# Another order of work in an attention block between two mixtures of experts: layer normalisations one pair later, reordered end of attention, a third batch gathered on TensorE

## The reference

```python
x = x + 0.5 * ffn(layernorm(x))     # "first experts"
x = x + attn(layernorm(x))          # "attention"
x = x + 0.5 * ffn(layernorm(x))     # "last experts"

def ffn(inputs):                    # 2048 tokens, 8 experts, 128 -> 512 -> 128
    probs = softmax(tokens @ gate_w.T); expert = argmax(probs)        # one expert for a token
    ranks = cumsum(one_hot(expert)) - 1                               # its place in the expert
    kept if rank < 320                                                # capacity
    h = relu(dispatched @ w1 + b1); out = h @ w2 + b2
    ans = probs * out, put back to the tokens' rows
def attn(states):                   # 16 heads of 64, causal
    q, k, v = (tanh(states @ W + bias) for each of Wq, Wk, Wv)
    return tanh(softmax(q @ k.T / 8, causal) @ v @ Wo + bo)
```

## Time and profile before

| | us |
|---|---|
| median of three runs | 459.39 |
| lowest and highest run | 458.07, 459.64 |
| the profiled execution | 458.94 |
| its span | 457.2 |
| TensorE busy in the span | 401.2 (88%) |
| VectorE busy | 322.0 (70%) |
| ScalarE busy | 247.8 (54%) |
| GpSimd busy | 207.7 (45%) |

### The profile page before, as it was taken

The page is one execution under the profiler, slowest core; times in us unless marked ns, Lnnn a source line. Parts: engine busy times, 40 slices in busy tenths (PEclk is TensorE's granted clock), DMA queues, the critical chain, the costliest instruction groups (busy, mean ns, idle before and its releaser), DMA issues.

```text
span 457.2 us, 11460 instructions
## 1 busy us (share of the span) xinstructions
PE 401.2 (88%) x4654; PEld 302.2 (66%) x4654; DVE 322.0 (70%) x852; ACT 247.8 (54%) x369; POOL 207.7 (45%) x176
## 2 busy tenths in 40 slices
PE   1689889758799999999999999999999989789992
PEld 0556556526677888587877687887678875346771
DVE  6789677836999786389799478889558886554321
ACT  2111444228476878387768377777468661224641
POOL 6665064254544444154443357453346544130546
PEclk9999999989899999999999999999999999979997
DMA  7912643208000000000000010000000000217531
GB/s 213 373 49 75 177 124 94 62 24 279 2 1 1 3 2 4 1 24 1 3 2 3 8 30 7 10 1 3 7 8 30 10 1 19 58 31 204 146 96 36
DMA packets 25372, 25.46 MB, mean 56 GB/s; under 512 B 2664, under 2 KB 21551, under 8 KB 25048
## 3 DMA queue, kind: packets, MB, share of 16 engines
q1 hardware_dynamic: 21424, 18.33, 13.7%
q0 software_dynamic: 2304, 4.25, 2.8%
q10 hardware_dynamic: 1592, 2.14, 1.3%
HBM read 16.72 MB, written 9.58 MB: 58 GB/s over the span
## 4 chain that ended last, share of the span: by engine, by line
PE 60%; DVE 26%; issue 9%; POOL 2%; ACTq 1%; DMA 1%; ACT 1%; POOLq 0%; DVEq 0%
PE sc L820 8%; PE sc L680 7%; DVE Pl L1317 7%; PE pj L689 7%; DVE Ph L1312 6%; PE pj L789 5%; PE tT L869 5%; PE cx L852 4%; PE cx L854 3%; PE cx L853 3%; PE pj L799 3%; PE tT L623 3%; PE pj L820 2%; PE pj L869 2%; DVE XN L994 1%
## 5 line engine op out<-in xcount | busy, mean ns | idle before, releaser
L820 PE MATMUL sc<-Tq,Tk 64*128 64x128 f32 (+2 forms) x640 | 78.6, 345 | 0.0
L852 PE MATMUL cx<-Vh,Ph 128*128 128x65 f16 x640 | 65.8, 196 | 10.5 <-DVE Pl L1317 5.0
L820 PEld LDWEIGHTS sc<-Tq,Tk 64*128 64x128 f32 x640 | 62.3, 187 | 11.6
L1312 DVE CAST Ph<-Pf 128x1024 f16<-128x1024 f32 (+1 forms) x48 | 49.3, 1028 | 29.2 <-ACT Pf L568 29.2
L852 PEld LDWEIGHTS cx<-Vh,Ph 128*128 128x128 f16 x640 | 58.6, 98 | 16.5 <-DVE cn L1326 5.2
L853 PE MATMUL cx<-Vl,Ph 128*128 128x64 f16 x640 | 65.6, 194 | 0.0
L854 PE MATMUL cx<-Vh,Pl 128*128 128x65 f16 x640 | 65.3, 194 | 0.0
L853 PEld LDWEIGHTS cx<-Vl,Ph 128*128 128x128 f16 x640 | 59.0, 99 | 0.3
L854 PEld LDWEIGHTS cx<-Vh,Pl 128*128 128x128 f16 x640 | 59.2, 98 | 0.0
L479 ACT ACTIVATE hT<-sc,RT 128x320 f32<-128x320 f32 x64 | 33.7, 527 | 35.4 <-PE sc L680 34.9
L1312 DVE CAST Ph<-Wf 128x1024 f16<-128x1024 f32 (+1 forms) x48 | 42.8, 892 | 4.8 <-ACT Wf L568 4.7
(11 more groups left out here) (237 smaller groups left out, 1050.5 us busy)
## 6 DMA issues: line engine op xcount, KB each, us to landing
W<-in_L_ffn_w SPq DMA_DIRECT2D x32, 256.0 KB, 2.9
disp<-empty SPq DMA_DIRECT2D x2, 1320.0 KB, 7.9
XE<-disp SPq DMA_DIRECT2D x18, 132.0 KB, 2.6
X<-xmid SPq DMA_DIRECT2D x4, 256.0 KB, 3.2
out<-X SPq DMA_DIRECT2D x4, 256.0 KB, 2.3
XR<-disp SPq DMA_DIRECT2D x18, 33.0 KB, 2.3
X<-in_L_attn_states SPq DMA_DIRECT2D x2, 256.0 KB, 3.3
X<-in_L_attn_states SPq DMA_DIRECT2D x1, 512.0 KB, 5.4
```

Source lines behind the costliest of these rows:

```text
L820: m = mm(score_bank(h, c)[:, o + x:o + y], Tk[u][half(h), q:q + P], Tq[u][half(h), q + x:q + y], start=False, stop=last and (c, h) != (2, 0))
L852: mm(cx[:, o:o + HD + 1], Ph[u][:, h, a:a + P], Vh[u][:, kt, h, :], start=kt == 0, stop=False)
L1312: dve.tensor_copy(Ph[u][:, :, at], Pf[u][:, :, at]).then_inc(S["p_hi"], 1)
```

## The change

It has four parts.

1. `experts` on VectorE: weight split and bias step stand ahead of `outputs(e)`, `normalise_rows(e + 4)` behind it; the split has 6 pieces of 512 columns instead of 8 of 384. In the first experts TensorE's `gather(1)` is done for batch 0 ahead of hidden(0), the rest behind it.
2. X_STATS, X_APPLY and X_TURN are one pair later, and batch 0's scaling of batch 1's rows too: the scaling stands behind the casts of a pair. The transposes of xa wait for their tile alone; the first two terms of kq wait for the high half XH alone.
3. The tail: the scores of the last pair ahead of the ranks; the projection in groups of inputs 0 to 3, 4 to 6 and 7 instead of 0 to 5, 6 and 7; the last context in PSUM bank sc; on VectorE the work on batch 2 (ranks, part, weights, places, low half, one-hot matrices) behind `normalise`; on GpSimd the dispatch of batch 2 behind the power of batch 3.
4. Last experts: batch 2 of experts 0 and 1 is gathered on TensorE too (`gather_group`), the part is of batches 0 and 1 alone (loads wait for 24 scatters) and is added in PSUM by matmuls with the identity, so that `keep_part` and the addition are gone. 6 filling matmuls remain of 20. TensorE starts with gather(0), gather(1), hidden(0), hidden(1), outputs(0), outputs(1).

```diff
-X_STATS, X_APPLY, X_TURN = {0: 1, 2: 2, 4: 3}, {1: 1, 3: 2, 5: 3}, {2: 1, 4: 2, 6: 3}
-LATE, SPLIT = 5, 384
+X_STATS, X_APPLY, X_TURN = {1: 1, 3: 2, 5: 3}, {2: 1, 4: 2, 6: 3}, {3: 1, 5: 2, 7: 3}
+LATE, SPLITS = 5, 6
...
-        NH = flat(CT[:, 0:2, :]).rearrange("p (t d) -> p t d", d=P)
-        NL = Pl[0][:].rearrange("p a n -> p (a n)")[:, 0:NT * P].rearrange("p (t d) -> p t d", d=P)
-        HOT = [flat(Pf0[:]).rearrange("p (t n) -> p t n", n=CAP), flat(CT[:, 2:7, :]).rearrange("p (t n) -> p t n", n=CAP)]
-        part = [Tq[e][:, 0:CAP] for e in range(2)]
...
+        PART = (NG - 2) * GT
+        NH, NL = [tile[:].rearrange("p (t d) -> p t d", d=P) for tile in (XH, XL)]
+        hot_first = [flat(tile).rearrange("p (t n) -> p t n", n=CAP) for tile in (Pf[0][:], CT[:, 0:5, :])]
+        hot_last = [flat(tile).rearrange("p (t n) -> p t n", n=CAP) for tile in (Pf[0][:], Pf[1])]
+        HOT = (hot_first, hot_last)
+        gbank = (pj1, cx)
...
-                            sp.wait_ge(S["scattered"], 16 * (2 * NT - GT))
+                            sp.wait_ge(S["scattered"], 16 * (NT + PART))
...
-            batch_dispatch(NG - 2)
             batch_inv_std(NG - 1)
             for e in range(2):
                 pool.wait_ge(xe_in[e], 32)
             pool.wait_ge(xr_in[0], 64)
+            batch_dispatch(NG - 2)
             batch_dispatch(NG - 1)
...
-            def keep_part():
-
-                act.wait_ge(S["part_ps"], 1)
-                act.activation(part[0], pj1[:, 0:CAP], ACT.Copy)
-                act.activation(part[1][:, MAIN:CAP], pj1[:, CAP:CAP + REST], ACT.Copy)
-                act.activation(part[1][:, 0:MAIN], sc[0][:, 0:MAIN], ACT.Copy).then_inc(S["part_ready"], 1)
...
+            split_n(2 * NG - 2, NG - 2)
...
-            def transpose_group(src, ps, done):
+            def transpose_group(src, ps, done, ready=None):
                 for t in range(GT):
+                    if ready:
+                        pe.wait_ge(ready[0], ready[1] + t)
                     last = nc.tensor.transpose(ps[:, P * t:P * t + P], src[:, t, 0:P], identf[:])
                 last.then_inc(done, 1)
...
+            def gather_group(phase, e, g):
+
+                since = g - NG + 2
+                done = NG + since + 1 if phase else g + 1
+                pe.wait_ge(S["n_hi"], done)
+                pe.wait_ge(S["n_lo"], done)
+                pe.wait_ge(S["hot_ready"], 2 * NG + 2 * since + e + 1 if phase else NG * e + g + 1)
+                for t in range(GT * g, GT * g + GT):
+                    begin, final = t == (PART if phase else 0), t == NT - 1
+                    mm(gbank[e][:, 0:CAP], NH[:, t, :], HOT[phase][e][:, t, :], start=begin, stop=False)
+                    last = mm(gbank[e][:, 0:CAP], NL[:, t, :], HOT[phase][e][:, t, :], start=False, stop=final)
+                if final:
+                    last.then_inc(S["xe_ps"], 1)
...
-                gather(0)
-                hidden(0)
-                gather(1)
-                outputs(0)
-                hidden(1)
+                if phase:
+                    gather(0, (NG - 1,))
+                    gather(1, (NG - 1,))
+                    hidden(0)
+                    hidden(1)
+                    outputs(0)
+                    outputs(1)
+                else:
+                    gather(0, range(NG))
+                    gather(1, (0,))
+                    hidden(0)
+                    gather(1, range(1, NG))
+                    outputs(0)
+                    hidden(1)
                 tokens(2)
                 for e in range(1, E - 2):
                     hidden(e + 1)
                     turn_back(e - 1)
                     tokens(e + 2)
-                    outputs(e)
+                    if e > 1 or not phase:
...
-                pe.wait_ge(S["xa_ready"], g + 1)
                 if g:
                     pe.wait_ge(S["x_lo"], g)
-                transpose_group(xa, tT, S["xa_ps"])
+                transpose_group(xa, tT, S["xa_ps"], (S["xa_ready"], GT * g + 1))
...
-                    pe.wait_ge(S["x_lo"], b + 1)
+                    pe.wait_ge(S["x_hi"], b + 1)
...
+                        if r == 0 and w and xl:
+                            pe.wait_ge(S["x_lo"], b + 1)
...
-                if c or h:
+                if bank is cx and (c or h):
...
-            step(NG, 0, project=False, route=lambda: rank_batch(NG - 2, cx), cx_read=(S["rank_read"], NS + NG - 1))
             pairs = NPAIR * NG
+            scores(pairs - 1, 1, False)
+            pe.wait_ge(S["ctxn"], 2 * (pairs - 3) + 2)
+            rank_batch(NG - 2, cx)
+            pe.wait_ge(S["rank_read"], NS + NG - 1)
+            context(pairs - 2, 0, 0)
+            context_t(pairs - 3, 1)
+            context(pairs - 2, 0, 1)
             pe.wait_ge(S["tv"], pairs)
-            project_out(NG - 1, pj0, 0, 6)
+            project_out(NG - 1, pj0, 0, 4)
+            context(pairs - 1, 1, 0)
             context_t(pairs - 2, 0)
-            context(pairs - 1, 1, 0)
-            context(pairs - 1, 1, 1)
-            project_out(NG - 1, pj0, 6, 7)
+            context(pairs - 1, 1, 1, sc[0])
+            project_out(NG - 1, pj0, 4, 7)
             context_t(pairs - 1, 1)
             project_out(NG - 1, pj0, 7, 8)
             turn_out(NG - 1)
-            keep_busy(20)
+            for e in range(2):
+                gather_group(1, e, NG - 2)
+            pe.wait_ge(S["part_in"], 1)
+            for e in range(2):
+                rest = slice(REST * e, REST * e + REST)
+                for j in range(2):
+                    mm(gbank[e][:, P * j:P * j + P], XM[e][:, j, :], identf[:], start=False, stop=False)
+                last = mm(gbank[e][:, MAIN:CAP], XMR[rest, :], identf[rest, rest], start=False, stop=False)
+            last.then_inc(S["part_ps"], 1)
+            keep_busy(6, sc[0])
             pe.wait_ge(S["x_added"], NG)
             turn_batch(NG - 1)
             route_logits(NG - 1, sc[1])
-            pe.wait_ge(S["part_in"], 1)
-            for j in range(2):
-                nc.tensor.transpose(pj1[:, P * j:P * j + P], XM[0][:, j, :], identf[:])
-                nc.tensor.transpose(sc[0][:, P * j:P * j + P], XM[1][:, j, :], identf[:])
-            nc.tensor.transpose(pj1[:, MAIN:MAIN + P], XMR[:], identf[:]).then_inc(S["part_ps"], 1)
             rank_batch(NG - 1, sc[3])
...
+                    for dst, at, n in ((0, 0, CAP),) if e == 0 else ((REST, 0, MAIN), (0, MAIN, REST)):
+                        last = dve.tensor_copy(xeT[e][:, dst:dst + n], gbank[e][:, at:at + n])
...
-                    part = slice(SPLIT * e, SPLIT * e + SPLIT)
+                    part = slice(512 * e, 512 * e + 512)
...
-                if between:
-                    between()
                 for e in range(E):
                     if e + 2 < E:
                         tokens(e + 2)
-                    if e + 4 < E:
-                        normalise_rows(e + 4)
+                    if e == 0 and between:
+                        between()
                     if phase == 0:
-                        split_weights(e)
-                    outputs(e)
-                    if not phase:
+                        if e < SPLITS:
+                            split_weights(e)
                         if e == 1:
                             bias_high()
                         if e == 2:
...
                             where()
                         if e == 5:
                             bias_rows()
+                    outputs(e)
+                    if e + 4 < E:
+                        normalise_rows(e + 4)
...
-            step(NG, 0, between=lambda: take_ranks(s, NS + NG - 2, GT * (NG - 2), 0, GT, cx))
-            place(s, GT * (NG - 2), 0, GT)
+            step(NG, 0, between=lambda: read_ranks(s, NS + NG - 2, 0, GT, cx))
+            normalise_part()
             normalise(NPAIR * NG - 1, 1, 0)
-            normalise(NPAIR * NG - 1, 1, 1)
+            normalise(NPAIR * NG - 1, 1, 1, sc[0])
+            weigh(s, NS + NG - 2, GT * (NG - 2), 0, GT)
+            place(s, GT * (NG - 2), 0, GT, near=True)
+            low_n(NG, NG - 2)
+            dve.wait_ge(S["spot_ready"], NS + 1)
+            for e in range(2):
+                hot(1, e, NG - 2)
             add_out(NG - 1)
             batch_stats(NG - 1)
             norm_batch(NG, NG - 1)
-            normalise_part()
-            low_n(NG, NG - 1)
+            low_n(NG + 1, NG - 1)
             s = Steps(dve, S["route_step"], ROUTE_STEPS * (NS + NG - 1), ROUTE_STEPS)
             choose(s, NS + NG - 1, 0, GT, sc[1])
             take_ranks(s, NS + NG - 1, GT * (NG - 1), 0, GT, sc[3])
             place(s, GT * (NG - 1), 0, GT, near=True)
-            dve.wait_ge(S["spot_ready"], NS + 1)
+            dve.wait_ge(S["spot_ready"], NS + 2)
```

90 lines of the change are left out of this document (40 added, 50 removed).

## The result

The changed kernel takes 451.32 us (median of four runs, 450.07 to 452.66), the kernel before on the same chip 458.81: a ratio of 0.984 (95% interval 0.980 to 0.987), or 7.5 us less. The profiled execution took 452.66, with a span of 450.6; it was the longest of the four. So the table has both.

A forecast was written before the change was run, and what follows sets the result against it. No single engine was taken to bound the kernel, so each stage was read by itself: 458.94 - 4.0 - 3.1 - 1.3 + 0.7 = 451.2 us. The range of 8 in 10 was 447.8 to 455.2.

The forecast's parts named there:

- First experts: VectorE's new order closes TensorE's holes before the hidden layers, and the earlier gather helps: 4.0 us less, bounds 0.9 and 4.4.
- The 0.3 for a full VectorE: First experts: 0.3 us taken off the gain because VectorE's own load is full at expert 2.
- First batch: Attention's first batch: normalisations one pair later remove VectorE's wait for GpSimd's power: 3.1 us less, between 2.1 and 3.7.
- one pair later the power runs beside the first pair's casts: First batch: GpSimd's power runs during VectorE's casts, saving 1.17 + 0.9 = 2.1 us, the lower end.
- Rival A: One large term missing (22%): first experts keep 0.9 of 4.0, 454.3, or first batch 1.0 to 2.1 of 3.1, 452.2 to 453.3.
- The port: First batch: by the skill's shared-port rule the power would block a cast about 1 us, making 3.1 2.1; forecast kept 3.1.
- Tail: Attention's tail: earlier last contexts, fewer small steps and a bank of its own, less projection matmuls moved behind: 1.3 us less.
- the 1 to spare: Tail: VectorE gets some 6 us of work ahead of the last addition, leaving about 1 us of its idle time.
- Last experts: Both gathers first close one hole, but the copy of expert 3 is uncovered: 0.7 us more, between 0 and 1.4.
- the charge of 1.5 for the copy that outputs(1) no longer covers: Last experts: before hidden(3), outputs(0), scaling, copy and hand-overs take 1.7 us against 0.22, so 1.5 more.
- Rival D: Batches 1 to 3: pairs fall into another rhythm where VectorE's subtraction meets GpSimd's each time: 467 us (4%).

The follow-up runs named there:

- e1_vector_order: Changed kernel with VectorE's order in the first experts alone put back (scaling, split, outputs, bias step): 455.99 us, 0.9925; 455.79 without one execution of 690.21.
- second profile: Profiled execution of a later run of the changed kernel, same code, another granted clock: 449.0 us, span 446.9; that run's median 452.53 us, 0.9859.
- b1_tables_alone: Kernel before with only the changed X_STATS, X_APPLY and X_TURN tables, third chip: 461.45 us, 0.9954.
- e7_before_fill: Kernel before with the same 13 filler matmuls ahead of its attention and nothing else, second chip: 463.81 us, 1.0009.
- g1_fill_again: Changed kernel with the 13 fillers, a second time, on the third chip: 452.28 us, 0.9741.
- e8_more_fill: Kernel of e4 with 9 more fillers, 5 while VectorE chooses batch 3's experts, 4 while it makes the last one-hot matrices: 450.74 us, 0.9725.
- e3: Changed kernel with 13 more matmuls nobody reads, 10 behind the first experts' last product, 3 behind the transposes of batch 0's rows: 449.76 us, 0.9795.
- e4: Changed kernel with the 13 fillers and, in the last experts, TensorE's outputs(1) back behind tokens(3): 450.33 us, 0.972.
- e5: Changed kernel with the 13 fillers and the three old X_STATS, X_APPLY and X_TURN tables put back: 455.49 us, 0.9814.
- e6_fill_tail: Changed kernel with the 13 fillers, old projection groups in the tail and the last context's second half in the first's bank: 452.2 us, 0.9746.

## Why the prediction was right, and where it was not

**First experts: right.** 4.0 was forecast, 3.93 came. The four periods took 19.49 by the starts in the timeline (50.20 to 69.69), 19.66 by those in the chain, where 19.42 was forecast. Hidden(1) came 0.4 sooner instead of 0.9 (47.23 to 46.79). The earlier gather gave its 1.1 (from hidden(0) to hidden(1) it is 7.56 us, 8.72 before), but hidden(0) came 0.7 later and not 0.2; how much of that is the gather is open, since hidden(0) starts anywhere from 38.72 to 41.37 in the profiles with this order. The 0.3 for a full VectorE wasn't needed, so two small misses cancel. e1_vector_order confirms the mechanism.

**First batch: right mechanism, missed condition.** The step that failed is "one pair later the power runs beside the first pair's casts", with the casts taken as ready at once. At the full clock the term is 3.5 (3.1 forecast, 3.7 the upper bound). In the first profile it is 0.93, under the lower bound of 2.1: the first scores ran at 1.2 GHz, and VectorE waited 2.86 us for them where it had waited for GpSimd. Rival A had this ("a pair that is served sooner only waits later"), and priced what it takes away at 1.0 to 2.1; in the first profile 2.17 went. Before, VectorE's scaling stood ahead of the casts and covered that delay; when it goes, the cover goes. The low clock of 93.2 to 96.6 in the kernel before was a cost that only waited for its cover to be taken away.

**The port.** The forecast set a rule of the Trainium skill ("SBUF — State Buffer", Who interferes with whom) against the row of a cast beside GpSimd's power. In the second profile the power ran from 102.61 to 104.03, and VectorE's two casts beside it took 1.29 together:

```profile
102.61 1.42 POOL L358 TENSOR_TENSOR r<-ve,mhalf 128x4 f32<-128x4 f32 x1 [1.32 <-DVE ve L999]
104.02 2.96 POOL L403 TENSOR_TENSOR Pl<-Pf,Ph 128x1024 f16<-128x1024 f32 x1
```

That is 0.65 for each, as 0.68 in the row of before. They weren't blocked, and the rows decided rightly. The third cast, from 104.90, took 2.36 beside GpSimd's large subtraction where it takes 0.42 alone; that one agrees with the rule.

**Tail: right on the first chip.** 1.3 forecast, 1.56 came in the first profile: 0.60 ahead of the first projection and 0.96 behind it. VectorE still idled 1.45 us ahead of the last addition, near the 1 to spare that was forecast, and GpSimd 3.47 ahead of its last dispatches, against 3.

On the other two chips it is worth more, which nobody forecast. From the keys of pair 31 to the last addition the changed tail takes 27.90 to 27.95 us on all three chips, where the clock isn't low in it; the old one takes 29.51 in before, 31.98 in b1_tables_alone on the third chip and 33.17 in e7_before_fill on the second. Of that, 2.0 us stand at one place, VectorE's `normalise` of the first half of the last context. Its first instruction in before, and below it the same one in b1_tables_alone:

```profile
385.54 0.18 DVE L1322 RECIPROCAL rden<-cx 128x4 f32<-128x4 f32 x1 [2.25 <-PE cx L854]
```

```profile
388.10 0.18 DVE L1322 RECIPROCAL rden<-cx 128x4 f32<-128x4 f32 x1 [4.27 <-remote]
```

TensorE's part was done at 386.04 in the second case, and e7_before_fill has the same 4.27. "remote" is a release for which the trace has no instruction, so what VectorE waited for stays open.

**Last experts: wrong by 0.9.** The hole of "near 2 us" before hidden(3) came as forecast (2.07). What failed is first the clock of the gathers. The forecast let the second gather run in part at the lower level, 1.1 to 2.2 us, as the first did in before; but in the first profile both ran at the upper level, 2.33 us for the two where one alone had taken 2.30. With the clock low over the gathers as in before, the changed order takes 41.05 from the indices to the last hidden layer (g1_fill_again), 0.6 more than the 40.49 before, near the 0.7 that was forecast; at the full clock 40.29 and 39.96, which is less. And second, the charge of 1.5 for the copy that outputs(1) no longer covers is right only at the low clock, where outputs(1) in its old place is worth 1.4. At the full clock TensorE is sooner done and would wait for the loads of experts 2 and 3: hidden(2) starts at 12.42 in e8_more_fill with outputs(1) not yet done, and at 13.42 in the first profile with its 2.15 us done, so more than half of it fills that wait.

**The sum.** The first profile lost 2.2 in the first batch and gained 0.9 in the last experts, which leaves it 1.3 above the forecast; and it was the longest of the four executions, 1.34 above their median. That the median meets the forecast to 0.1 us is luck, though three of the four terms are right in mechanism and near in size in one profile or the other. Rival D did not come: from pair 8 to pair 31 it is 200.70 to 200.76 us in all traces of the first chip and 201.03 to 201.18 on the others, with the old tables and the new.

## What to carry to other kernels

Where a wait is removed, ask what else it covered: here a slow stretch of the clock ahead of it cost nothing while another engine was later, and 2.6 us once that engine was early. So read the granted clock of every stretch that feeds the place, not only of the stretch itself, and price a term at both levels. And an uncovered hole is only a cost if the engine could have been there sooner: look for the transfer that sets the next start. Compare two traces of a stage only where the clock takes the same course in both.

## What was not expected of the hardware

The granted clock takes different courses in the same kernel: low from 89.6 to 103.2 us in one execution and from 89.1 to 92.5 in another, with the same code. The span differs by 3.7 us (450.6 and 446.9). The 13 fillers went with the upper level ahead of the first scores in five profiles (e3, e4, e5, g1, e8), but not in e6_fill_tail (low from 94.8 to 98.2) nor in e7_before_fill; and e1_vector_order had the upper level there without them. The kernel before was also some 4 us longer on the second and third chip (463.6 and 463.4 against 459.2), while the changed kernel was not (452.15 against 452.53), so the ratio was 0.984 and 0.986 in two measurements and 0.976 on the third chip. The traces show a part of the reason: the old tail takes 2.5 us longer in b1_tables_alone and 3.7 in e7_before_fill than in before, and the changed tail the same on all three chips. Whether it is the chip or the hour can't be told, as the second and third chip were each measured once, and the changed kernel as it is did not run on the second.
